# A scan and a transformer block on one core: the scan's first 32 steps computed ahead, idle matrix products behind later steps, and a new order of work

## The reference

```python
px = einsum('btc,dc->btd', x, W_state) + b_state
g  = sigmoid(einsum('btc,dc->btd', x, W_gate) + b_gate)
def step(state, inp):
    p_t, g_t = inp
    state = tanh(p_t + state)
    return state, g_t * state
```

## Time and profile before

| | |
|---|---|
| median of 3 runs | 1593.18 us |
| profiled execution, its own time | 1590.76 us |
| its span, first to last instruction | 1589.0 us |
| TensorE busy | 1393.2 us, 88% |
| VectorE busy | 69% |
| ScalarE busy | 60% |
| GpSimd busy | 20% |
| mean granted TensorE clock | 0.928 |

### The profile page before, as it was taken

The page is one execution under the profiler, slowest core; times in us unless marked ns, Lnnn a source line. Parts: engine busy times, 40 slices in busy tenths (PEclk is TensorE's granted clock), DMA queues, the critical chain, the costliest instruction groups (busy, mean ns, idle before and its releaser), DMA issues.

```text
span 1589.0 us, 33614 instructions
## 1 busy us (share of the span) xinstructions
PE 1393.2 (88%) x12320; PEld 1104.4 (70%) x12320; DVE 1096.9 (69%) x2884; ACT 951.8 (60%) x2090; POOL 317.6 (20%) x1146
## 2 busy tenths in 40 slices
PE   6905779999976799999999999999999899998997
PEld 3404668889863467778886577866787467875797
DVE  7867486655577967777888766787788667864242
ACT  2535465676555687777565846458544684567931
POOL 3343232223333323322332100001000100000000
PEclk9956579999985889999998999999999999999998
DMA  5584136855654445736666555574756556665443
GB/s 167 147 287 128 35 98 189 259 170 153 197 185 147 130 144 153 222 120 214 203 196 200 163 172 167 187 235 147 226 185 188 180 160 211 188 196 190 126 131 112
DMA packets 235572, 274.35 MB, mean 173 GB/s; under 512 B 36624, under 2 KB 158992, under 8 KB 235152
## 3 DMA queue, kind: packets, MB, share of 16 engines
q1 hardware_dynamic: 235408, 272.19, 56.2%
HBM read 229.98 MB, written 43.45 MB: 172 GB/s over the span
## 4 chain that ended last, share of the span: by engine, by line
PE 64%; DVE 10%; ACT 9%; DMA 7%; issue 4%; POOL 2%; SPq 2%; ACTq 0%; DVEq 0%; POOLq 0%
PE PS L1054 60%; ACT work L1008 3%; PE PS L1057 3%; DMA KT<-ktd 3%; POOL AD L1729 2%; ACT PX L940 2%; PE PS L1138 2%; SPq L862 1%; DVE mx L1528 1%; ACT work L1033 1%; DMA UU<-in_L_attn_x 1%; DMA work<-in_L_ffn_e_l 1%; DVE st L1340 1%; DMA ktd<-KTs 1%; DMA WB<-wlo_e_l 1%
## 5 line engine op out<-in xcount | busy, mean ns | idle before, releaser
L1729 POOL TENSOR_TENSOR AD<-PX 128x8 f32<-128x8 f32 x1023 | 247.7, 242 | 564.7 <-ACT PX L940 548.6
L940 ACT ACTIVATE PX<-AD 128x8 f32<-128x8 f32 x1023 | 219.3, 214 | 230.2 <-POOL AD L1729 227.6
L1008 ACT ACTIVATE work<-PS 128x1024 f32<-128x1024 f32 (+1 forms) x312 | 288.9, 960 | 85.9 <-PE PS L1054 84.7
L1528 DVE TENSOR_REDUCE mx<-PS 128x2 f32<-128x1024 f32 (+3 forms) x224 | 252.3, 1143 | 84.7 <-PE PS L1054 84.3
L1054 PE MATMUL PS<-work,vlx 128*32 128x256 f32 (+2 forms) x2816 | 240.8, 385 | 21.4 <-ACT work L1008 8.5
L1054 PE MATMUL PS<-EP,u_e_l 128*128 128x256 f32 x1024 | 193.7, 284 | 1.6 <-DVE EP L1388 1.4
L1736 POOL TENSOR_SCALAR_AFFINE_SELECT work<-work 128x512 f32<-128x512 f32 x96 | 65.0, 687 | 628.2 <-ACT work L1008 628.2
L1054 PE MATMUL PS<-WB,work 128*128 128x192 f32 x1024 | 182.6, 333 | 4.2 <-ACT work L1033 2.9
L1033 ACT ACTIVATE work<-PS 128x512 f32<-128x512 f32 x176 | 104.4, 597 | 127.6 <-PE PS L1054 125.9
L1054 PE MATMUL PS<-EP,WB 128*128 128x256 f32 x640 | 180.0, 281 | 0.0
L1054 PEld LDWEIGHTS PS<-WB,work 128*128 128x128 f32 x1024 | 167.5, 192 | 10.6 <-issue 6.2
(11 more groups left out here) (175 smaller groups left out, 2345.0 us busy)
## 6 DMA issues: line engine op xcount, KB each, us to landing
KT<-ktd SPq DMA_DIRECT2D x112, 512.0 KB, 4.7
WB<-wlo_e_l SPq DMA_DIRECT2D x160, 256.0 KB, 3.0
WB<-wlo_e_up SPq DMA_DIRECT2D x64, 256.0 KB, 3.1
WB<-wlo_e_w SPq DMA_DIRECT2D x64, 256.0 KB, 3.0
ktd<-KTs SPq DMA_DIRECT2D x112, 128.0 KB, 2.6
WB<-wdn_e_down SPq DMA_DIRECT2D x64, 192.0 KB, 2.5
KT<-ktd SPq DMA_DIRECT2D x48, 256.0 KB, 4.1
KT<-ktd SPq DMA_DIRECT2D x32, 384.0 KB, 4.2
```

The source lines that it names most:

```text
L940: eng.activation(cur, AD[n % 2], ACT.Tanh).then_inc(of(*key), 1)
L1008: eng.activation(pt[:, :, :, q0:L], two("sc", *a).rearrange("p a (l q) -> p a l q", l=2)[:, :, :, q0:L], ACT.Exp).then_inc(of(*key), 1)
L1528: eng.tensor_reduce(o, x, AX, ALU.max, negate=True).then_inc(of(*key), 1)
L1729: eng.tensor_tensor(AD[n % 2], PX[c % 2][:, :, :, t], PX[(n - 1) // L % 2][:, :, :, (n - 1) % L], ALU.add).then_inc(of(*key), 1)
```

## The change

It has three parts.

1. The first tile of piece 0 is now the first 32 time steps of all four batches, not 128 steps of one batch (piece 0 is loaded by four DMAs per part, one per batch). That tile goes ahead under keys of its own (`xinf`, `hstf`, `hscf`, `htrf`, `hcpf`, `hpxf`, `houtf`), and the other three tiles (96 time steps) follow as piece 0. Steps 0 to 31 of the scan wait for `houtf` alone. In the planner, piece 0's `hst` comes behind `houtf`.
2. After planning, `stay_awake` walks TensorE's list and puts `spin` groups in its planned gaps between 76 and 880 us: up to 6 products of 128x256 bf16 whose result nobody reads, written into a PSUM bank that is free at that time. Each group waits for one scan step n (`stanh`) and for the readers of that bank. A group is left out where the planned work nearby already keeps TensorE busy (`ENOUGH`).
3. The due times (`START`, `AT`) and the planner's costs of switching (`STAY`) are replaced, and `LOW` goes to 0, so that the planner's TensorE is never slow.

```diff
+AWAKE, SPIN, SPAN, ENOUGH = (76.0, 880.0), 0.107, 3.4, 0.8
-WINDOW, LOW, HIGH, FRESH = 3.413, 0.38, 0.75, 80.0
+WINDOW, LOW, HIGH, FRESH = 3.413, 0.0, 0.75, 80.0
-STAY = {"pe": 24.2, "act": 5.7}
+STAY = {"pe": 30.8, "act": 16.0}
-START = (101.2, 162.6, 177.3, 239.6, 336.5, 416.5, 521.4, 595.3, 735.9, 806.3, 936.0, 1005.2, 1113.3, 1190.3, 1307.3, 1390.6)
+START = (93.6, 160.7, 167.8, 222.0, 363.3, 420.4, 549.5, 576.5, 742.0, 794.6, 944.4, 987.9, 1088.8, 1180.6, 1294.1, 1388.4)
-AT = {"piece": (-133.2, 84.2, 12.4, 109.4),
+AT = {"piece": (-191.8, 101.3, 151.7, 166.3),
...
+def stay_awake(P):
...
+    seen = [(over(("stanh", n)), n) for n in range(1, T)] + [(1e6, T)]
+    for i, k in enumerate(pe):
+        e0, s1 = (P.start[pe[i - 1]] + P.took[pe[i - 1]] if i else 0.0), P.start[k]
+        while seen[at][0] < max(e0 - 0.3, AWAKE[0]):
+            at += 1
+        while seen[at][0] < min(s1 - 0.35, AWAKE[1]):
+            t, n = seen[at]
+            at += 1
+            room = min(seen[at][0], s1) - max(t, e0) - 0.2
+            near = sum(max(0.0, min(b, t + 0.6 * SPAN) - max(a, t - 0.4 * SPAN)) for a, b in streams)
+            count = min(6, int(room / SPIN))
+            bank = open_bank(max(t, e0))
+            if near > ENOUGH * SPAN or count < 1 or bank is None:
+                continue
...
+            order.append(key)
+        order.append(k)
...
+    add("sp", ("xinf",), 1.4, -20.0, lat=3.5)
+    add("dve", ("hstf",), 2.3, -20.0, ("xinf",))
+    add("dve", ("hscf",), 0.42, -20.0, ("hstf",))
...
+        add("dve", ("hst", n), 3.75 if n else 3.4, d, ("xin", n), *([] if n else [("houtf",)]))
...
-        px = [("hout0", 2 * c + t // 128)] if c < 2 else [("pxl", c)]
+        px = [("houtf",)] if n < 32 else [("hout0", 2 * c + t // 128)] if c < 2 else [("pxl", c)]
...
-    return P.run()
+    return stay_awake(P.run())
...
+                elif kind == "xinf" or key == ("xin", 0):
+                    for b in range(B):
+                        x = A["L0_attn_x"][b, 0:128, :].rearrange("(i t) d -> t i d", t=32)
+                        i = slice(0, 1) if kind == "xinf" else slice(1, 4)
+                        eng.dma_start(half(0)[32 * b:32 * b + 32, i, :], x[:, i, :]).then_inc(of(*key), 16)
...
+                if kind == "spin":
+                    n, count = a
+                    for x in freed(key, "P0"):
+                        pe.wait_ge(*x)
+                    pe.wait_ge(*done("consts"))
+                    pe.wait_ge(*done("stanh", n))
+                    for i in range(count):
+                        mm(PS[:, place[key, "P0"], 0:256], identb, maskk.rearrange("p l q -> p (l q)"), True, True)
+                    continue
...
+                elif kind == "hpxf":
+                    pe.wait_ge(*done("wl", "x0"))
+                    pe.wait_ge(*done("hcpf"))
+                    for m in range(2):
+                        for kc in range(2):
+                            ins = mm(one(*key)[:, 128 * m:128 * m + 128], wx[:, kc, 128 * m:128 * m + 128], normed(0)[:, kc, 0:128],
+                                     kc == 0, kc == 1)
...
+                elif kind == "houtf":
+                    for m in range(2):
+                        src = one("hpxf")[:, 128 * m:128 * m + 128].rearrange("p (b t) -> p b t", b=B)
+                        ins = eng.tensor_scalar(PX[0][:, m, :, 0:32], src, bx[:, m:m + 1], None, ALU.add)
```

More of the change, by code:

```diff
@@ L211, in run, with open_bank @@
         return self
+def stay_awake(P):
+    pe = P.order["pe"]
+    streams = [(P.start[k], P.start[k] + P.items[k][1]) for k in pe]
+    over = lambda k: P.start[k] + P.took[k] + P.items[k][5] + HOP
+    takes = defaultdict(list)
+    for (k, p), i in P.place.items():
+        for j in range(i, i + BANKS.get(p, 0)):
+            takes[j].append((P.start[k], P.items[k][3][p]))
+    for j in takes:
+        takes[j].sort(key=lambda x: x[0])
+    def open_bank(t):
+        best = None
+        for j in takes:
+            before = [x for x in takes[j] if x[0] < t]
+            last = max((over(x) for x in before[-1][1]), default=0.0) if before else 0.0
+            if last < t and (best is None or last < best[0]):
+                best = (last, j, before[-1][1] if before else ())
+        return best
+    seen = [(over(("stanh", n)), n) for n in range(1, T)] + [(1e6, T)]
+    order, at = [], 0
+    for i, k in enumerate(pe):
[11 more added lines that the diff above has]
+                continue
+            key = ("spin", n, count)
+            P.items[key] = ("pe", count * SPIN, 0.0, {}, "128", 0.0)
+            P.feeds["stanh", n].append(key)
+            P.start[key], P.took[key] = max(t, e0), count * SPIN
+            P.place[key, "P0"], P.turn[key, "P0"] = bank[1], bank[2]
+            streams.append((max(t, e0), max(t, e0) + count * SPIN))
+            order.append(key)
+        order.append(k)
+    P.order["pe"] = order
+    return P
 def tiles_of_time(u):
@@ L278, in arrange @@
         add("sp", ("wdd", w), 0.35, 80.0, lat=6.0)
+    add("sp", ("xinf",), 1.4, -20.0, lat=3.5)
+    add("dve", ("hstf",), 2.3, -20.0, ("xinf",))
+    add("dve", ("hscf",), 0.42, -20.0, ("hstf",))
+    add("pe", ("htrf",), 0.25, -20.0, ("hscf",), ("ident",), mode="128",
+        take={"P1": (("hcpf",),), "xnT": (("hpx0", 0), ("hpx1", 0))}, lat=DRAIN)
+    add("dve", ("hcpf",), dve(256), -20.0, ("htrf",))
+    add("pe", ("hpxf",), 0.9, -20.0, ("hcpf",), ("wl", "x0"), mode="128", take={"P1": (("houtf",),)}, lat=DRAIN)
+    add("dve", ("houtf",), 0.62, -20.0, ("hpxf",), ("wl", "bs"))
     for n in range(2 * NCH):
@@ L935, in _ @@
                     if n == 0:
[L936 removed]
+                        act.wait_ge(*done("houtf"))
                         eng.activation(cur, cur, ACT.Tanh).then_inc(of(*key), 1)
@@ L1066, in _ @@
                         pe.wait_ge(*x)
-                if kind == "htr":
+                if kind == "spin":
[7 more added lines that the diff above has]
+                    continue
+                if kind == "htrf":
+                    pe.wait_ge(*done("ident"))
+                    pe.wait_ge(*done("hscf"))
+                    for kc in range(2):
+                        ins = tr(one(*key)[:, 128 * kc:128 * kc + 128], half(0)[:, 0, 128 * kc:128 * kc + 128])
+                    ins.then_inc(of(*key), 1)
+                elif kind == "htr":
                     n, i = a
-                    ps = two("htr", n, 0)
+                    first = 0 if n else 1
+                    ps, col = two("htr", n, first), 128 * (i - first)
                     pe.wait_ge(*done("ident"))
@@ L1079, in _ @@
                     pe.wait_ge(*done("hcp", n))
-                    xn = xnT[place[("htr", n, 0), "xnT"]]
+                    if n == 0:
+                        pe.wait_ge(*done("hcpf"))
+                    done_before = 0 if n or gate else 128
                     for m in range(2):
@@ L1723, in _ @@
                     c, t = divmod(n, L)
-                    if c < 2:
+                    if n < 32:
+                        pool.wait_ge(*done("houtf"))
+                    elif c < 2:
                         pool.wait_ge(*done("hout0", 2 * c + t // 128))
```

128 lines of the change are left out of this document (78 added, 50 removed).

## The result

The changed kernel took 1614.32 us, the median of 4 runs (1610.81 to 1617.13), beside 1593.29 us for the kernel before (4 runs, 1586.98 to 1593.67): ratio 1.014, 95% interval 1.0108 to 1.0173. The forecast of 1559 was wrong in sign, and 1614 lies outside its range. The profiled execution took 1613.33 us (span 1611.6), at a granted clock of 0.965 (before 0.928).

A forecast was written before the change was run, and what follows sets the result against it. TensorE bounds the kernel, losing time in two troughs made by the scan. Terms -10.6 - 5 - 9 - 10.4 + 3 = -32 took 1590.8 to 1559 us; main case 1542 to 1577 (chance 0.60), wider range 1530 to 1592.

The forecast's parts named there:

- The lead, -10.6: Head: with the first 32 steps ahead, the scan begins at 13.2 us instead of 23.8, saving 10.6 us.
- VectorE: four tiles took ... for one tile ... 2.3: Head: VectorE's statistics, aggregates and small operations for the first tile take 2.3 us instead of 3.97, ending at 7.1.
- Ends 4 us later: Head: TensorE's stream of other products, which fills it to 81 us, ends 4 us later, delaying the last gate store.
- Everything downstream is shifted by -10.6: After the head: the scan's earlier start moves all later work, and so the end, 10.6 us earlier.
- The clock, -5, -9 and -10.4: Half-clock TensorE work from 80 to 240, 440 to 560 and after 560 us: savings of 5, 9 and 10.4 us.
- At 2.4 GHz each sum would at best halve: Half-clock stretches: TensorE's busy sums of 57.6, 38.3 and 20.7 us would at best halve at full clock.
- The third term: After 560 us TensorE is full, so half of its 20.7 us at half clock is saved: -10.4 us.
- The idle products, +3: TensorE's gaps: groups delay early work by 3 us, bounds 0 and 53, since most planned gaps end as planned.
- The order, 0, bounds -15 and +15: New due times across the kernel: given nothing beyond the -5 for 80 to 240 us, bounds -15 and +15.
- TensorE is held by the scan: Rival, chance 0.14: groups waiting for scan steps block TensorE's strict list, giving 1614 us.
- The products do not hold the clock: Rival, chance 0.14: groups leave holes at every step, the clock stays low, only the lead is left: 1583 us.
- Everything pays: Rival, chance 0.12: all 117 half-clock us are halved, with the lead and the +3: 1525 us.

The follow-up runs named there:

- e7: Kernel before with its own lists, GpSimd's scan additions left out so each tanh no longer waits for the step before: 1586.88 us, ratio 0.9944.
- e10: Kernel before with its own lists, VectorE's maxima of the scores reading only half of their columns: 1592.88 us, ratio 0.9968.
- e2: Kernel before, lists and head unchanged, with 620 idle products put in its planned gaps: 1594.69 us, ratio 0.9987.
- e5: Changed kernel with the statistics and scalings of piece 1 moved behind `houtf` in VectorE's list: 1621.23 us, ratio 1.0153.
- e1: Changed kernel with the same new lists and head but without its idle products: 1616.01 us, ratio 1.0104.
- e6: Kernel before with its old lists plus the new head alone, scan steps moved 13 places earlier, no idle products: 1602.98 us, ratio 1.0033.
- e12: Changed kernel with 160 more idle products in TensorE's planned gaps after 880 us: 1615.84 us, ratio 1.0103.
- e9: Changed kernel's new lists and head without idle products and without the scan's additions, so no chain: 1610.43 us, ratio 1.0094.
- e3: Changed kernel with idle products that no longer wait for a scan step: 1609.47 us, ratio 1.0102.

## Why the prediction was wrong

**What bounds the kernel.** That TensorE idles in two troughs and that the scan's gates stand at their ends was read rightly. That a microsecond saved there is a microsecond of time was not shown by it. e7, e10 and e2 relieve the scan, VectorE and TensorE's clock in turn, and bring 9 to 11, 5 to 6 and 1 to 2 us, the last not told apart from nothing. I take the reason to be that every engine follows a fixed list in strict order, made with the old durations, so that what is ready sooner waits at its old place; no run tested this by itself.

**The lead, -10.6.** The first tanh came at 15.63, not 13.2. The failed step is "VectorE: four tiles took ... for one tile ... 2.3": I costed the first tile's operations but not VectorE's list between them. The statistics of piece 1 (8.66 in the timeline) stand ahead of the copy (12.34), and the product at 12.90 waits for the copy, not for the weights that I had named as late. With piece 1's statistics moved away (e5) it does wait for the weights, which land at 9.45 (10.4 in the prediction), and the first tanh comes at 12.21: the term's other parts were sized well. "Ends 4 us later" for the head's other products was 12.5 us (93.3 for 80.8), because the head's stream now has gaps (such as 2.00 us at 76.76), and the store was late by that much. Some 4 of the 12.5 are the clock: in this execution TensorE is at half clock from 49.5 to 52.9 and from 76.8 to 80.2 us, which falls on the eight products behind that gap (5.37 us for 3.67 in e1); e1's stream ends at 89.2, and that of e6, with the old lists, at 86.0. "Everything downstream is shifted by -10.6" failed outright: the lead is 7.4 us at step 127, gone at step 383, 2.7 at step 511 and negative at the end. In e1's profiled execution it is 11.4 at step 127 and 11.1 at step 511, unit 4 is gated at 405.62 where the prediction had 406, and yet its span is 11.9 us longer than before. So the step that failed is not only that the lead was lost on its way to the gate of unit 4, but that a lead there was taken for time at the end. Alone, the head gave +0.3% (e6), and an earlier first tanh nothing (e5). Even the scan without its chain, 17 us ahead at step 127, gained only 9 to 11.

**The clock, -5, -9 and -10.4.** "At 2.4 GHz each sum would at best halve" was a bound, and the terms then took it as the value. Matched one by one in e2, products took 1.64 times as long at half clock, which gives back 0.39 of their time; over the whole kernel it was 0.35. The Trainium skill's page TensorE: Matmul & The Clock Gate (section HAM oscillation — how this bites in real kernels) also counts half of the throttled time as the penalty. An estimate by that page gives 27.6 us for the 55.2; the trace of e2 gives 19.2. The Trainium skill's section Single matmul latency on the same page gives the latency of a single bf16 product a constant part that is only about 10% longer at the lower clock. The lengths of the float32 records above agree in kind, since none of them doubles. My three terms together were 24.4 us of time at the end. TensorE's busy time did fall by 19.2 in e2, but the end did not move (ratio 0.9987), so what failed is that this time would reach the end. Whether it lay beside the path or was given back behind the groups is not shown, as said above. The third term did not come at all: after 560 us the changed kernel is still at half clock for some stretches (0.96 and 0.97), since only 34 idle products lie between 560 and 880, and the 160 more of e12 left the clock after 880 where it was (0.96 and 0.99 for 0.97 and 0.98).

**The idle products, +3.** "Most end as planned if the rest does" had no row behind it: in e2 work stood ready behind a group in 49 of 75 places, some 20 us, and the bound of 53 held that. How much of it reached the end is not shown. With the sizes measured in e2, -19.2 + 23.5, the clock and the idle products together are worth +4 us in its profiled execution and nothing by the medians, where I had -21.4.

**The order, 0, bounds -15 and +15.** The term that was put at nothing without a row failed too. From e6 to e1, ratio 1.0033 to 1.0104, the new lists cost 0.7% or 11 us (the two ran on different chips, and the intervals touch at 1.0053); from e7 to e9, where the head is changed too, 1.5%. The bounds held. What failed is the thought that the order could be priced by what it leaves room for. Moves of up to 2 us in its numbers cost 75 and 129 us.

The account of +21 us is thus about +6 for the head (e6) and +11 for the lists (e1 against e6), if the head costs in the new lists what it costs in the old ones, which no run shows; the remaining 4 are not told apart from 0, since the intervals of e1 and of the changed kernel overlap. Which places of the new lists cost the 1% stays open. Candidates in the trace are the wait of 5.89 us for a weight load at 245.82 and the stretch from 880 to 1200, where TensorE is 7.6 us less busy than before and the clock is 0.97 for 0.99; no run tested them.

**The rivals.** "TensorE is held by the scan" had named 1614, and the number came by luck, not by its mechanism. It asked for over 30 us of waits on the tanh; there are 14.9, e3 without them is no faster beyond its interval, and e1 without any idle product takes the same time. Its cousin, real work ready behind a group, is real, and with the clock's gain it comes to nothing in e2. "The products do not hold the clock" is refuted by the windows (0.65 to 0.97). The trace does not agree with the rule cited for it from the Trainium skill: with the groups in place e2 has 2 half-clock stretches of 20.5 us in all between 85 and 240 us, where there had been five of 112.6. "Everything pays" is refuted by e2. Of the signs, the mean clock over 0.97 was 0.965, unit 0's transpose near 93 was 102.07 and unit 4 near 406 was 414.0; of those for being wrong, the changed kernel has half-clock stretches from 175.8 to 186.1 and from 244.1 to 250.9 us, and the scan does not stall at step 32.

## What to carry to other kernels

Idle work placed in the gaps of a strict queue can stand in front of real work that has become ready. Its gain is to be sized by products matched at both clocks (here 0.39 of their time, and about a third of the half-clock time over the whole kernel), and counts only where TensorE's speed moves the end: here it paid in one pair of seven, where 123 us of half-clock work went away. Before counting a saved resource as time, test with one cheap experiment whether relieving it moves the end at all: in the lists of the kernel before, neither the clock, nor the scan's chain, nor 13% of VectorE's work was worth over about 0.7%. In a kernel whose lists were searched, new due times are a new draw, and their effect is measured against neighbouring draws on the chip, not argued.

## What the runs showed of the hardware

At 1.2 GHz float32 products of 512 and 256 columns took 785 and 439 ns for 483 and 320 at nearly full clock, factors of 1.63 and 1.37 for single records. From start to start in unbroken streams the factors were 1.48 (transposes of 128x128), 1.81 (products of 128x256) and 1.96 (of 128x192). The same 511 products kept TensorE busy 80.3 us at half clock (before) and 48.9 at full clock (e2); over whole kernels a microsecond of half-clock TensorE time less went with 0.26 to 0.38 us less busy time. In the head of the changed kernel eight float32 products behind a gap of 2.00 us took 5.37 us, partly at half clock, and 3.67 in e1 at full clock. With the idle products in TensorE's gaps the granted clock from 80 to 240 us rose from 0.65 to 0.94, and the time of the kernel stayed (ratio 0.9987).
